# Graph layer pair on one core: tensor-engine picks cover 96 of 128 slots, and the attention terms share the outgoing sums' memory

## The reference, cut to what matters

```python
h = (x_flat @ W_gat).reshape(M, HEADS, NUM_EXPERTS)       # 16 values a node
a_src = (h * att_src).sum(-1)                              # 4 a node
a_dst = (h * att_dst).sum(-1)                              # 4 a node
e = leaky_relu(a_src[src] + a_dst[dst], negative_slope=0.2)
e_max = segment_max(e, dst); ee = exp(e - e_max[dst])
denom = segment_sum(ee, dst)
agg = segment_sum(h[src] * alpha[:, :, None], dst) + b_gat # alpha = ee / denom[dst]
...
for ei in range(NUM_EXPERTS):
    g = where(topk_i == ei, w, 0.0).sum(-1)
    hh = gelu(x @ W1[ei] + b1[ei], approximate=False)
    out = out + g[..., None] * (hh @ W2[ei] + b2[ei])
```

## Time and profile before

| what | value |
| --- | --- |
| time, median of 3 runs | 5029.56 us (5017.0 to 5035.1) |
| the profiled execution's own time | 5033.03 us |
| its span | 5031.2 us |
| mean granted TensorE clock | 0.892 |
| PE busy | 4040.3 us (80%) |
| DVE busy | 2481.3 us (49%) |
| ACT busy | 1049.4 us (21%) |
| POOL busy | 592.7 us (12%) |

### The profile page before, as it was taken

The page is one execution under the profiler, slowest core; times in us unless marked ns, Lnnn a source line. Parts: engine busy times, 40 slices in busy tenths (PEclk is TensorE's granted clock), DMA queues, the critical chain, the costliest instruction groups (busy, mean ns, idle before and its releaser), DMA issues. The chain is left out here.

```text
span 5031.2 us, 88369 instructions
## 1 busy us (share of the span) xinstructions
PE 4040.3 (80%) x24382; PEld 2921.8 (58%) x24433; DVE 2481.3 (49%) x6896; ACT 1049.4 (21%) x2087; POOL 592.7 (12%) x667
## 2 busy tenths in 40 slices
PE   3888755799879989765998950897978889979999
PEld 1333324466468669533775630796953379846766
DVE  5999978899720121145552125203035556533333
ACT  0133331222130110211113310200001134323333
POOL 1000001100000000000777740000011100000000
PEclk9999985787789899986999975899989989989999
DMA  2011220222234125101122333442520000010000
GB/s 97 38 64 71 79 83 0 76 83 80 69 128 150 70 78 192 56 3 19 41 59 57 37 47 125 147 173 82 198 75 0 0 1 0 3 22 13 13 13 25
DMA packets 134059, 322.81 MB, mean 64 GB/s; under 512 B 47723, under 2 KB 85135, under 8 KB 119466
## 3 DMA queue, kind: packets, MB, share of 16 engines
q1 hardware_dynamic: 117742, 300.20, 17.1%
q0 software_dynamic: 14000, 10.47, 2.2%
q10 hardware_dynamic: 2224, 11.01, 0.5%
HBM read 246.14 MB, written 76.96 MB: 64 GB/s over the span
## 5 line engine op out<-in xcount | busy, mean ns | idle before, releaser
L533 PE MATMUL ps<-hot_key,hot_src 128*126 128x512 bf16 (+1 forms) x2208 | 451.8, 317 | 44.9 <-DVE hot_key L500 21.0
L500 DVE TENSOR_SCALAR hot_key<-col_iota,edge_key,neg_group 128x625 bf16<-128x625 int16 x1104 | 486.0, 440 | 0.0
L2084 POOL DMA_INDIRECT fetched<-node_table,src_idx x384 | 398.6, 1038 | 126.7 <-issue 126.7
L533 PEld LDWEIGHTS ps<-hot_key,hot_src 128*126 128x126 bf16 x2208 | 211.9, 135 | 276.3 <-DVE hot_key L500 242.2
L1241 PE MATMUL ps<-gnn_u_thirds,near 125*128 125x256 bf16 x3000 | 337.0, 275 | 23.2 <-issue 23.2
L1241 PEld LDWEIGHTS ps<-gnn_u_thirds,near 125*128 125x128 bf16 x3000 | 330.8, 141 | 27.6 <-issue 24.9
L498 DVE TENSOR_SCALAR hot_src<-col_iota,src_low 128x125 bf16<-128x125 int16 x1104 | 280.8, 254 | 39.1 <-PE ps L533 34.7
L2189 PE MATMUL ps<-xnT,ew 128*128 (+2 forms) x640 | 185.7, 446 | 75.0 <-ACT ehT L2274 57.5
L2691 PE MATMUL ps<-prod,v_apart 125*99 125x512 f32 x416 | 201.1, 640 | 40.6 <-DVE prod L2569 40.6
L756 PE MATMUL ps<-row_hot,slot_hot 128*128 128x512 f16 x1088 | 228.9, 362 | 3.5 <-DVE row_hot L915 2.0
L2909 PE MATMUL ps<-scores_kv,phi_cols 128*125 128x33 f32 (+1 forms) x1800 | 223.1, 270 | 0.1
(11 more groups left out here) (530 smaller groups left out, 6776.2 us busy)
## 6 DMA issues: line engine op xcount, KB each, us to landing
near<-adjacency SPq DMA_DIRECT2D x80, 1562.5 KB, 6.6
adjacency<-counts SPq DMA_DIRECT2D x125, 312.5 KB, 2.2
own_in<-own_rows SPq DMA_DIRECT2D x34, 512.0 KB, 4.0
expert_rows<-rows_y SPq DMA_DIRECT2D x100, 125.0 KB
pair_in<-high_rows SPq DMA_DIRECT2D x34, 256.0 KB, 4.9
pair_in<-low_rows SPq DMA_DIRECT2D x34, 256.0 KB, 5.5
agg0a_adj<-adjacency SPq DMA_DIRECT2D x5, 1562.5 KB, 9.4
spare<-adjacency SPq DMA_DIRECT2D x5, 1562.5 KB, 9.5
```

Of the source, the lines that this page charges most:

```text
L500: nc.vector.tensor_scalar(hot_key[:, j, :], col_iota[:], edge_key[:, ds(chunk, 1)], neg_group[:, ds(group, 1)], ALU.subtract, ALU.is_equal ...
L533: last = nc.tensor.matmul(sums[:, b:e], hot_src[:, j, :], hot_key[:, j, b:e], start=False, stop=True, skip_group_check=True)
L2084: pool.indirect_dma_start(out=fetched[:, q, j, :], out_offset=None, in_=node_table, in_offset=bass.IndirectOffsetOnAxis(ap=src_idx[:, q, j ...
```

## The change

`TURNED` goes from 64 to 96, so that the tensor engine picks 96 of the 128 slots of blocks 0 and 1, in 12 pieces of 8 slots instead of 8, and POOL gathers 32 slots of each instead of 64. The buffers for keys and masks grow with it. To make room, `gap` lies in the memory of `dst_in`, and `terms` in that of `sums_out`. Because of the latter DVE's wait for the last store moves: it now stands ahead of the terms, 25 instructions before its old place.

```diff
-TURNED = 64
+TURNED = 96
 GPIECE = 8
 GPIECES = TURNED // GPIECE
...
-                    gap = s("gap", [128, 4, SLOTS])
+                    gap = dst_in
                     weight_in = s("weight_in", [128, 4, SLOTS])
                     sums = s("gsums", [128, ACCS, SLOTS + 1])
                     sums_out = s("sums_out", [128, SLOTS, ACCS])
-                    terms = s("terms", [128, 16, SLOTS])
+                    terms = sums_out[:].rearrange("p s n -> p (s n)")[:, 0:16 * SLOTS].rearrange("p (n s) -> p n s", s=SLOTS)
...
                         step(nc.vector.tensor_tensor(decay[:], decay[:], same[:].unsqueeze(1).to_broadcast([128, 4, SLOTS]),
                                                      ALU.mult))
+                        dve.wait_ge(out_stored, b * 16 + 16)
                         for h in range(4):
                             step(nc.vector.tensor_tensor(
...
                         step(nc.vector.tensor_copy(sums[:, :, 0:1], sums[:, :, SLOTS:SLOTS + 1]))
-                        dve.wait_ge(out_stored, b * 16 + 16)
                         step(nc.vector.tensor_copy(row_out_i[:], row_out_f[:]))
```

## The result

The changed kernel takes 5047.81 us in the median of five runs (5043.51 to 5052.1), where the kernel before now stands at 5028.70 (five runs, 5015.69 to 5035.1). The ratio is 1.0037 with a 95% interval of 1.0024 to 1.0050: 0.4% slower. The interval leaves 1 out, so the loss is real, but it lies inside the 0.5% that count as no change here. 5049.3 was predicted.

A forecast was written before the change was run, and what follows sets the result against it. POOL's gathers bound the stage before; 57.5 us added on PE's stream, less waits saved, makes ACT's last weigh set its end 19.7 us later. The profiled 5033.0 becomes 5052.7, the median 3.4 lower: 5049.3 us, range 5036 to 5061.

The forecast's parts named there:

- What removes: POOL's queue: 64 gathers, 83.2 us less to issue, but only 7.1 us ahead because its store waits for DVE.
- What adds: PE's stream, blocks 0 and 1: four more pieces each, 28.2 and 29.0 us, plus 0.3 for the mask, 57.5 in all.
- The keys: Keys' broadcast growing from 2 to 3 MB: landing 14.0 us after issue, just in time, cost 0 or up to 1 us.
- The moved wait: DVE's wait for the last store, now before the terms: cost 0, with 0 to 2 us as bounds.
- The sum: Step-by-step total from POOL and ACT to the stage's end: last weigh and all behind it 19.7 us later.
- (b): ACT at block 2's weigh: 7.45 us of waiting and 0.5 us of cold start saved, leaving a delay of 49.6 us.
- R1: Added pieces cheaper than PE's rows: ACT arrives earlier, break-even at 4.7 us a piece, at best 4994 us; chance 0.12.
- x: Time in us per block of added pieces; ACT reaches the last weigh at 2908.1 + 2x, break-even at 18.7.
- R2: POOL's queue binds alone, so all 83 us of removed gathers come off: 4946 us; chance 0.02.
- R3: Pieces run at PE's lower clock: 5106 us, a tenth of it 5055, a fifth 5061; chance 0.13 with other large additions.
- R4: DVE's new wait for a store before the terms binds in four blocks: 5059 us with 2.4 us overrun; chance 0.03.

The follow-up runs named there:

- run 5: Kernel before without 64 gathers of blocks 0 and 1, no picks instead: 5391.07 us, ratio 0.9879; repeated on another chip: 5032.02 us, ratio 0.9996.
- run 6: Changed kernel with PE multiplying two of the table's three bf16 parts, 64 matmuls a piece for 96: 5416.58 us, ratio 0.9947 to the kernel before.
- run 2: Changed kernel with TURNED back at 64, leaving only the shared memory and the moved wait: 5027.92 us, ratio 0.9999 to the kernel before.
- run 1: Changed kernel with ACT's last weigh one group earlier in expert 3: 5030.86 us, ratio 1.0006 to the kernel before.
- run 4: Changed kernel with TURNED = 80 and the last weigh one group earlier: 5103.49 us, ratio 1.0148 to the kernel before.
- run 3: Changed kernel with TURNED = 80 and the old order of weigh: 5112.16 us, ratio 1.0166 to the kernel before.
- run 7: Changed kernel with TURNED = 80, but the keys' DRAM buffer kept at 96 rows: 5111.90 us, ratio 1.0165 to the kernel before.
- run 8: Changed kernel with TURNED = 80, and POOL repeating 12 of its last gathers: 5130.43 us, ratio 1.0202 to the kernel before.
- run 10: Changed kernel with 80 slots, earlier last weigh and 64 matmuls on zeros before the second layer's attention output: 5441.56 us, ratio 1.0007 to the kernel before.
- run 11: Kernel before with 64 matmuls on zeros ahead of the second layer's attention output: 5449.37 us, ratio 1.0014.
- run 9: Changed kernel with 80 slots, earlier last weigh and 24 matmuls on zeros before the second layer's attention output: 5064.48 us, ratio 1.0099 to the kernel before.

## Why the prediction was right

**What removes.** Forecast: POOL ahead by 7.1 us and not by 83, since its store waits for DVE. Measured 7.6, with 81.87 us of waiting (some 80 forecast). Shown by itself in run 5: the stage gets 33.2 us shorter, and that is the whole worth of the removal. By block 3 the lead had shrunk: DVE had its scores ready for ACT at 2941.0, where 2938.4 was forecast. That cost nothing, since ACT came later still, but it is why DVE's last wait for weights was 24.88 us and not 29.

**What adds.** 28.2 and 29.0 us forecast, 28.35 and 29.80 measured, and 0.24 for the mask (0.86 for 0.62) where 0.3 was taken. Up to block 2's `weigh` the delay, counted from the stage's start, is 58.2 us for 57.5. The granted clock was 1.00 and 0.97 as before:

```profile
2439.70:2524.40 84.70, 84.66 (x1154) 83.53 (x1153) 59.94 (x110) 0.38 (x1) 36.39 (x36) 1.00 0.07 9
2572.80:2660.50 87.70, 87.60 (x1153) 86.32 (x1154) 61.20 (x113) 0.00 (x0) 67.59 (x67) 0.97 0.12 13
```

The figure was right and its reason half right: I took PE as the one that paces a piece. Run 6 has DVE at the same 7.07 us by itself. The figure holds whichever of the two paces, since PE's row already ran at DVE's pace; so the wrong reason cost nothing here.

The 84.71 us for 1152 matmuls are 73.5 ns each. The isolated gap worked out in the prediction from the Trainium skill ("TensorE: Matmul & The Clock Gate", section Back-to-back issue gap), an estimate of 72.5 ns, stays a little low. It would not have shortened a piece, since DVE needs 7.07 us for one.

**The keys.** They landed 11.0 us after their issue at the slowest of two, not 14.0; DVE had its first compare at 2434.87, PE began at 2439.67. Counted from the stage's start PE began 0.2 us later than before. No cost, as taken. The formula of the Trainium skill ("DMA: Bandwidth & Descriptors", section Anatomy of one DMA) is a fit for DMAs issued from GpSimd, and this one is issued by SP. Its estimate of 9.2 us is too short here, where 9.5 and 11.0 were measured.

**The moved wait.** 0 forecast, 0 measured (run 2).

**The sum.** Saved in (b): the 7.45 us, and 2.1 us in the group behind it where 0.5 was forecast. From first Gelu to first row copy it took 10.42 us now (2819.08 to 2829.50) for 12.58. I had taken block 1's 12.07 as the price without a cold start, but the clock was low there too: PE waited 2.76 us at 2650.75 and 2.75 us at 2819.66, and shortly after PE had gone on, the granted clock fell the first time and not the second. Kernel before, then the changed one:

```profile
2650.00:2655.00 5.00, 4.25 (x10) 2.90 (x11) 4.90 (x4) 1.80 (x5) 3.85 (x4) 0.66 0.11 9
2770.00:2775.00 5.00, 5.00 (x11) 3.30 (x12) 4.86 (x5) 1.21 (x3) 4.09 (x4) 0.57 0.11 13
```

```profile
2819.00:2824.00 5.00, 4.34 (x17) 3.07 (x18) 4.90 (x4) 2.57 (x6) 3.85 (x4) 1.00 0.14 10
```

On the path that sets the end, that is the one term that was mis-sized by more than 1 us. Why the clock fell once and not the other time is not shown. So `weigh` came 18.8 us later, counted from the stage's start, where 19.7 was forecast, and the stage's end 18.1. The span's 19.1 for 19.7 is closer than the steps are, since 1.0 us from other stages stands in it; that much is chance. That ACT's arrival sets the end is shown by run 1. That the gathered rows come right behind it shows in run 4, where ACT waits for the scores again.

**The rivals.** R1 did not come: ACT does not wait. Its own formula held up at x of about 14 us: 8 to 10 us forecast (run 3), 10.4 measured in the stage. R2 is refuted by run 5 (33.2 us of the stage, not 83). R3: the clock in the pieces held, at 1.00 and 0.97. R4: refuted by run 2, and the terms of the changed kernel list no idle time either. What no rival of mine had is that the time of a later stage can go by 40 to 90 us with an edit that does not touch it. That it did not strike the changed kernel itself is luck: the prediction had nothing to say on it, and the same effect put run 3, with 80 slots, 84 us above the kernel before. The changed kernel's attention output took 296 us as before (4092.7 to 4388.7 as against 4076.5 to 4372.5, first to last start of L2909).

**What stays open.** What decides when the clock rises in the second layer's attention output. Not the DRAM layout by `key_rows` (run 7), not the moment alone (run 8). It came after 25 us (both kernels, runs 1, 2, 6, 10 and 11), 113 and 134 (the two traces of run 5's kernel, on two chips), 134 (run 9) and 223 us (runs 3, 4, 7 and 8). PE's idle time just ahead of the stage was 10.1 us in the four traces with 223, and 10.4 in those of both kernels and of runs 1 and 2, but 10.4 also in run 5's, so this difference does not settle it. The times of run 5 (seven executions near 5032 and one at 4982.9) and of run 9 suggest that one kernel can show two of these in different executions; the others were not profiled. `TURNED` also changes the places of the buffers in the core's own memory and the length of the programs, and neither was held fixed in a run.

## What to carry to other kernels

Moving work from a queue that is the bound is worth only what stands between it and the next wait in program order: look which store or signal that queue must pass, and who makes it. Here 83 us of issues were worth 33. The price was 58 us on PE's stream, which ACT follows, and ACT had only 37 us of waits to give. Then check where the once waiting engine has its hand-over: a single reorder on ACT was worth 17 us, nearly as much as the change had cost. And read the stage as well as the total, since a gain of 10 us in the edited stage can stand beside a loss of 90 in another, by another mechanism.

## What the runs showed of the hardware

The attention output of the second layer runs its transposes and 33-column matmuls at 50 of 50 us busy, and yet stays at 1.2 GHz for 25 to 223 us before it rises; in the windows read it then held 2.4 GHz. The stage is 296 to 391 us long accordingly. PE had stood idle for 10.1 to 10.4 us ahead of it, in runs 9 to 11 for 2.9 to 4.9 us behind the zeros. In the routed stage two waits of PE of 2.76 and 2.75 us, between the same instructions, went with a clock of 0.66 over 5 us in one kernel and of 1.00 in the other.

In three sets of runs the kernel before took 5027 to 5029 us, on two other chips 5442 and 5447. In the traces from those two the routed stage is 969 us (the first run 5), 1015 (run 6), 1038 (run 10) and 1042 us (run 11) long, for 631 of the kernel before on the others. It begins between 2376 and 2384, as everywhere. In run 6 ACT stood 124.7 us ahead of its copies of rows for something that the profile lays to none of this core's engines, and SP took 26.94 us over its first five stores of rows, which are 9.63 in the kernel before. The cause was not found. The change itself was not timed there, so its +0.4% holds for the first kind.
